# An attention kernel on one core: the small steps of gate and scales, and the masking of x, put into other batches

## The reference

```python
B, C, H, W = x.shape                       # 8, 512, 32, 32
pooled = jnp.mean(x, axis=(2, 3))
g = jax.nn.relu(pooled @ w1 + b1) @ w2 + b2
p = jax.nn.sigmoid(g)
mask = (p > 0.5).astype(x.dtype)
m = mask[:, :, None, None]
hyp_feat = x * m
euc_feat = x * (1.0 - m)
hyp_out = _logmap0(_mhsa(_expmap0(hyp_feat), hdn_w_qkv, hdn_b_qkv, hdn_w_o, hdn_b_o))
euc_out = _mhsa(euc_feat, eu_w_qkv, eu_b_qkv, eu_w_o, eu_b_o)
return hyp_out + euc_out
...
x = x + _L0_conv_ref(_gn(x), 1000, ...)    # _gn: group norm, 32 groups
```

## Time and profile before

| | us |
|---|---|
| median of 3 runs | 4210.61 (4202.07 to 4213.55) |
| the profiled execution: its time | 4202.53 |
| its span, first to last instruction | 4200.8 |
| PE busy in the span | 4004.4 (95%) |
| DVE busy | 2661.3 (63%) |
| POOL busy | 2693.4 (64%) |
| ACT busy | 1951.2 (46%) |

### The profile page before, as it was taken

The page is one execution under the profiler, slowest core; times in us unless marked ns, Lnnn a source line. Parts: engine busy times, 40 slices in busy tenths (PEclk is TensorE's granted clock), DMA queues, the critical chain, the costliest instruction groups (busy, mean ns, idle before and its releaser), DMA issues.

```text
span 4200.8 us, 68956 instructions
## 1 busy us (share of the span) xinstructions
PE 4004.4 (95%) x21822; PEld 2409.9 (57%) x21822; DVE 2661.3 (63%) x2643; ACT 1951.2 (46%) x3529; POOL 2693.4 (64%) x1311
## 2 busy tenths in 40 slices
PE   4899999999999999999999999999999999999999
PEld 3556565565655656556565555656556565555655
DVE  5565855658566684666746577465774657656585
ACT  4354534545345453454535445254553545435453
POOL 4474775747667486665857558574685746857477
PEclk9999999999999999999999999999999999999999
DMA  7212131121311213112141111311113111131212
...
DMA packets 143726, 306.49 MB, mean 73 GB/s; under 512 B 17248, under 2 KB 30048, under 8 KB 133088
## 3 DMA queue, kind: packets, MB, share of 16 engines
...
## 4 chain that ended last, share of the span: by engine, by line
PE 84%; DVE 9%; issue 4%; DMA 1%; ACT 1%; POOL 1%; SPq 0%; DVEq 0%; ACTq 0%; POOLq 0%
PE aux_ps L1220 30%; PE acc_ps L1331 20%; PE score_ps L1317 19%; PE aux_ps L1269 8%; PE score_ps L1220 4%; DVE mxp L1093 3%; PE aux_ps L1341 3%; DVE den L1154 1%; PE aux_ps L1278 1%; DVE o_t L1159 1%; DMA xin<-in_x_dram 1%; DVE sc L1000 0%; DVE keep L970 0%; DVE small L947 0%; DVE sc L907 0%
## 5 line engine op out<-in xcount | busy, mean ns | idle before, releaser
L628 POOL TENSOR_TENSOR sums<-sums,probs 128x1024 f32<-128x1024 f32 x768 | 1865.9, 2430 | 811.4 <-ACT probs L800 771.1
L1093 DVE TENSOR_REDUCE mxp<-aux_ps 128x2 f32<-128x1024 f32 x1031 | 1262.7, 1225 | 1094.6 <-PE aux_ps L1269 1068.7
L800 ACT ACTIVATE probs<-score_ps 128x512 f32<-128x512 f32 x2048 | 1056.5, 602 | 723.3 <-PE score_ps L1317 713.6
L1331 PE MATMUL acc_ps<-probs,v_y 128*64 128x512 f32 x4096 | 997.0, 608 | 0.0
L1220 PE MATMUL aux_ps<-xs,w_qk 128*128 128x512 f32 x3072 | 830.9, 408 | 0.0
L1220 PEld LDWEIGHTS aux_ps<-xs,w_qk 128*128 128x128 f32 x3072 | 542.3, 188 | 384.3 <-issue 267.9
L628 POOL TENSOR_TENSOR sums<-probs 128x1024 f32<-128x1024 f32 x128 | 305.0, 2383 | 501.3 <-ACT probs L800 501.3
L1269 PE MATMUL aux_ps<-k_hi,q_hi 64*128 64x512 f32 x2062 | 473.9, 453 | 102.5 <-DVE mxp L1093 100.7
L1331 PEld LDWEIGHTS acc_ps<-probs,v_y 128*64 128x64 f32 x4096 | 249.4, 136 | 468.4 <-issue 418.3
L1154 DVE RECIPROCAL den<-den 128x256 f32<-128x256 f32 (+1 forms) x240 | 443.9, 1850 | 7.7 <-ACT den L811 7.7
L1317 PE MATMUL score_ps<-q_hi,k_hi 64*128 64x512 f32 x2048 | 407.8, 394 | 17.9 <-issue 17.9
...
## 6 DMA issues: line engine op xcount, KB each, us to landing
...
xin<-in_x_dram SPq DMA_DIRECT2D x256, 256.0 KB, 2.9
...
```

The costliest lines, as they stand in the source:

```text
L628: pool.tensor_tensor(sums[h][:, :], a, probs[:, g % SLOTS_P, :], ALU.add).then_inc(c_sum[h].sem, 1)
L800: act.activation(probs[:, n % SLOTS_P, token_half(u % 2)], score_ps[:, u % SCORE_BANKS, :], ACT.Exp, scale=SCALE).then_inc(c_exp.sem, 1)
L1093: dve.tensor_reduce(mxp[:, :, n, h], ps, AX.X, ALU.max).then_inc(c_free["D"].sem, 1)
L1331: last = nc.tensor.matmul(acc_ps[head(j), :], v_y[:, m, head(2 * p + j)], probs[:, n % SLOTS_P, token_half(j)], start=(m == 0), stop=(m == ...
```

## The change

Four things are changed.

- The small steps of half 0 stand in other batches: statistics in 1 to 3 and none in 0, the group variance's product in 6 (was 5), the steps of the reciprocal deviation in 9, 10 and 11 (two of its parts now both in 9), the hidden layer in 12, the gate in 14, `ABOVE` in 17 (was 14), the masks (`KEEP`) in 25 (was 23) and `SHIFT` in 29.
- In half 1 the series is cut into five parts in batches 8, 9, 12, 13 and 14, and `BLEND` stands in 15 (was 14).
- The eight chunks of x go through by `MASK_AT`, in batches 15 (one), 16 (two), 17 (one), 19 (one), 20 (two) and 21 (one). ACT masks at the end of that batch, DVE scales a batch later, ACT makes the high part two batches later and POOL the low part at the start of the third.
- The ring has four buffers; the room comes from `squares`, whose work now alternates between two slots of `probs`, and from a narrower `mxw`.

```diff
-XIN = 3
+XIN = 4
-GATE_BATCH = {4: "mean", 5: "var", 11: "hidden", 13: "gate"}
-STATS_AT = {0: (0, 1), 1: (2, 3), 2: (4, 5), 3: (6, 7)}
-AGGREGATE, DEVIATIONS, RSTD_IN, RSTD, RELU, ABOVE, KEEP, SHIFT = 3, 5, 7, (8, 9, 10), 12, 14, 23, 24
+GATE_BATCH = {4: "mean", 6: "var", 12: "hidden", 14: "gate"}
+STATS_AT = {1: (0, 1, 2), 2: (3, 4, 5), 3: (6, 7)}
+AGGREGATE, DEVIATIONS, RSTD_IN, RSTD, RELU, ABOVE, KEEP, SHIFT = 3, 5, 7, (9, 10, 11), 13, 17, 25, 29
-CLAMP, POWER, SERIES, ROOT, NORM, EXP, SCALES, BLEND = 7, 8, (8, 11, 12), (9, 10), 11, 12, 13, 14
-OPERAND = [15, 16, 17, 18, 19, 20, 21, 22]
+CLAMP, POWER, ROOT, NORM, SERIES, EXP, SCALES, BLEND = 7, 8, (9, 10), 11, (8, 9, 12, 13, 14), 12, 13, 15
+MASK_AT = {15: (0,), 16: (1, 2), 17: (3,), 19: (4,), 20: (5, 6), 21: (7,)}
...
-        squares = sb("squares", [P, HALF])
-        mxw = sb("mxw", [P, NT, 66], F32R)
+        mxw = sb("mxw", [P, HD + NT], F32R)
...
             def x_lo(i, t, b):
-                if b - 1 in OPERAND:
-                    j = OPERAND.index(b - 1)
+                for j in MASK_AT.get(b - 3, ()):
...
                     for b in range(BATCHES):
+                        x_lo(i, t, b)
                         for g in (2 * b, 2 * b + 1):
...
                         if phase_at(b, MULT) is not None:
                             mult(phase_at(b, MULT))
-                        x_lo(i, t, b)
...
-                if b in OPERAND:
-                    operand_hi(i, t, OPERAND.index(b))
+                for j in MASK_AT.get(b, ()):
+                    mask(i, t, j)
...
                             exps(g)
-                        mask(i, t, b)
...
+                        for j in MASK_AT.get(b - 2, ()):
+                            operand_hi(i, t, j)
                         project(b)
...
-                if part < 2:
-                    root(i, part, small[:, 3, :], small[:, 2, :], small[:, 6, :])
+                    for n in range(2):
+                        root(i, n, small[:, 3, :], small[:, 2, :], small[:, 6, :])
...
-                if b in OPERAND:
-                    scale_x(i, t, OPERAND.index(b))
+                for j in MASK_AT.get(b - 1, ()):
+                    scale_x(i, t, j)
```

More of the change, by code:

```diff
@@ L75 @@
 RECIP, RECIP_PARTS = [6, 8], 4
+XIN_FIRST = ({"stats": 0, "w": 8, "operand": 12}, {"norm": 20, "operand": 28, "y": 36})
+NUMBERS = [first + j for kinds in XIN_FIRST for kind, first in kinds.items() for j in range(2 if kind == "w" else 8)]
 def max_slot_at(b, j):
@@ L394, in chunk_in, with y_square @@
             q = n % XIN
-            loads = (n - q) // XIN + 1
+            loads = 1 if t < 0 else len([c for c in NUMBERS if c <= n and c % XIN == q])
             eng.wait_ge(c_xin[q].sem, c_xin[q].at(i, 16 * loads))
             return xin_slot(t, kind, j)
+        def y_square(k):
+            return probs[:, SLOTS_P - 2 + k % 2, 0:HALF]
         def x_chunk(j):
@@ L413, in chunk_at @@
                 return 1 + j
-            first = ({"stats": 0, "w": 8, "operand": 10}, {"norm": 18, "operand": 26, "y": 34})[t]
-            return first[kind] + j
+            return XIN_FIRST[t][kind] + j
         def chunk_read(eng, i, t, kind, j):
@@ L539, in _ @@
                     if t:
-                        load_chunks(i, 1, "norm", range(5, 8), next_image)
-                        load_chunks(i, 1, "operand", range(3), next_image)
+                        load_chunks(i, 1, "norm", range(6, 8), next_image)
+                        load_chunks(i, 1, "operand", range(4), next_image)
                     load_qk(t, 3, 0)
@@ L675, in power, with mask @@
                 act.activation(dst, dst, ACT.Exp, scale=e).then_inc(made.sem, 1)
-            def mask(i, t, b):
-                if b in OPERAND:
-                    j = OPERAND.index(b)
-                    k, a = x_chunk(j)[0], 0 if new_image(t) else 1
-                    chunk = chunk_in(act, i, t, "operand", j)
-                    act.activation(chunk, chunk, ACT.Identity, bias=shift[:, a, k:k + 1],
-                                   scale=keep[:, a, k:k + 1]).then_inc(c_xm.sem, 1)
+            def mask(i, t, j):
+                k, a = x_chunk(j)[0], 0 if new_image(t) else 1
+                chunk = chunk_in(act, i, t, "operand", j)
+                act.activation(chunk, chunk, ACT.Identity, bias=shift[:, a, k:k + 1],
+                               scale=keep[:, a, k:k + 1]).then_inc(c_xm.sem, 1)
             def rstd_in(i):
@@ L899, in series @@
                 terms = [c / coefs[-1] for c in coefs[-2:0:-1]]
-                for n in ((0, 1), (2,), (3,))[part]:
-                    step(i, dve.scalar_tensor_tensor(dst, dst if n else s, terms[n], s, ALU.add, ALU.mult))
-                if part == 2:
+                if part < len(terms):
+                    step(i, dve.scalar_tensor_tensor(dst, dst if part else s, terms[part], s, ALU.add, ALU.mult))
+                else:
                     step(i, dve.tensor_scalar(dst, dst, coefs[-1], coefs[0], ALU.mult, ALU.add))
@@ L1069, in y_scale_step @@
                     step(i, dve.tensor_scalar(ss[:, :], ss[:, :], 1.0, None, ALU.min))
-                    for part in range(3):
+                    for part in range(5):
                         series(i, part, sc[:, 1, :], ss[:, :], ATANH_SERIES)
```

42 lines of the change are left out of this document (23 added, 19 removed).

## The result

The changed kernel takes **4165.7 us** (median of 4 runs, 4162.8 to 4168.1), the kernel before, run between them on the same chip, 4209.1 (4202.1 to 4213.6). The ratio is 0.990, with a 95% interval of 0.988 to 0.992. The forecast was 4192, with 4166 to 4214 as its range: the sign is right, the time lies 0.3 us under the range, and the gain is more than twice what was forecast. The two profiled executions say the same: spans of 4200.8 and 4161.1 us, 39.7 less, where the sum had 18. By the ratio's interval the gain is 36 to 50 us.

A forecast was written before the change was run, and what follows sets the result against it. PE, busy 95% at full clock, bounds the kernel with its work plus waits. Half 0 gains 4.2 us an image, half 1 loses 1.9: 18 for eight, 4202.5 to 4184; the runs' median lies 8 higher, 4192, range 4166 to 4214.

The forecast's parts named there:

- The rule of a wait: PE makes a batch's second pair of maxima only after DVE read the first; a read late by L costs L less 0.35.
- half 0's leaving costs: Half 0, per image: batch 5's wait of 2.3 to 2.5 us, batch 15's 1.0 and batch 24's 2.7 go.
- L955 in batch 10 and the multiplication in 11: Half 0: L955 behind batch 10's reciprocal keeps batch 11's 0.8 us; the last multiplication, behind batch 11's low part, costs 0.4.
- POOL's chain: POOL's low parts end 1.9 us later; in half 0 PE waits 1.3 in batch 20 and 1.0 in 24.
- Two scalings in a batch: Half 1, batches 17 and 21: two scalings delay the next read, costing 1.4 us in 18 and again in 22.
- Statistics leave batch 0, worth under 0.3 an image.: Half 0: moving the statistics out of batch 0 gains under 0.3 us an image.
- the change doesn't touch those: Waits of 0.7 and 1.2 us in the two batches 0, from the loop's turn and the last y tile's squares, stay.
- the ring's fourth buffer: Buffers for x: the fourth one, with the alternating squares, costs nothing, as no DMA held PE in the image shown.
- the series' parts in batches 9 to 14: Half 1: one more series step in batch 9 costs 0.3 to 0.5 us; one fewer in 11 wins 0.3.
- rival 1: The change does what it says and POOL's chain holds nobody: 5.8 us an image gained, 4164 us; chance 0.15.
- Rival 2: Slower: half 1's scalings in 18 and 22 miss a POOL sum, net loss 1.7 us an image, 4224 us; chance 0.14.
- rival 3: Nothing moves: half 1's new waits reach their upper bounds against the gate's savings, 4206 to 4210 us; chance 0.21.

The follow-up runs named there:

- e4: The kernel before with only half 0's statistics and the gate's steps moved, masks and half 1 as before: 4141.6 us, ratio 0.984.
- e8: The changed kernel with each ACT mask right behind the batch's exponentials, as in the kernel before, instead of at the batch's end: ratio 0.986.
- e7: The changed kernel with half 0's eight chunks of x back to one a batch, from batch 14 on: ratio 0.987.
- e9: The changed kernel with half 1's chunks one a batch, masks from batch 14 on and scalings from 15: ratio 0.988.
- e1: The kernel before with half 0's statistics alone moved to batches 1, 2 and 3: ratio 0.996.
- e2: The changed kernel with the statistics alone back in batches 0 to 3: ratio 0.994 to the kernel before.
- e3: The kernel before with the ring's fourth buffer, loads regrouped for it, squares in `probs` and the narrow `mxw`: ratio 0.998.
- e5: e4 with the ring's fourth buffer, the squares in `probs` and the narrow `mxw`: 4124.0 us, ratio 0.981 to the kernel before.
- e11: The kernel before with the squares in `probs` and the narrow `mxw`, but three buffers as before: ratio 1.000.
- e10: The changed kernel with half 1's small steps (series, `BLEND`) back where they stood before: ratio 0.989.
- e12: e5 with half 0's first five chunks one batch earlier and none worked on in batch 19: 4122.0 us, ratio 0.980 to the kernel before.

## Why the prediction was right or wrong

**Held.** *The rule of a wait and half 0's leaving costs*: batches 5, 15 and 24 lost 2.5, 1.0 and 2.7 us (e4), forecast 2.3 to 2.5, 1.0 and 2.7. `KEEP` in 25 and `ABOVE` in 17 hold nobody. *L955 in batch 10 and the multiplication in 11*: batches 10 to 14 together cost 0.5 an image more, forecast 0.4, and the wait in 11 stayed; but the 0.4 was to be a wait of PE in 12, and PE is idle there for 0.03 only, so the sum came right without its reason.

*POOL's chain*: PE waited 1.34 in image 3's batch 20, forecast 1.3, and 1.0 in 24, forecast 1.0. Counted from the start of batch 17 the chain to chunk 3 ended 2.0 later than before, forecast 1.9. The chain of the kernel after, POOL from batch 19 on:

```profile
1758.83 2.41 POOL L637 TENSOR_TENSOR sums<-sums,probs 128x1024 f32<-128x1024 f32 x1
1761.20 2.97 POOL L611 TENSOR_TENSOR xs<-xin,xs 128x512 fp32r<-128x512 f32 x2
1764.13 4.87 POOL L637 TENSOR_TENSOR sums<-sums,probs 128x1024 f32<-128x1024 f32 x2
1768.94 1.27 POOL L611 TENSOR_TENSOR xs<-xin,xs 128x512 fp32r<-128x512 f32 x1
```

and the q tile that starts when it ends:

```profile
1770.27 1.67 PE L1235 MATMUL aux_ps<-xs,w_qk 128*128 128x512 f32 x6 [1.34 <-POOL xs L611]
```

Of the 1.9 by which the chain was to end later, e8 showed the 0.7 of ACT's mask (0.65 came back), and with the chunks one a batch (e7) PE's wait for POOL in half 0 is gone.

*Two scalings in a batch*: forecast 1.4 in 18 and in 22, measured 1.43 and 1.34, and e9 took both away. DVE in batch 17 of half 1 (the two scalings, 2.49 and 2.89 by their single rows, and the read they delay):

```profile
2001.88 5.30 DVE L1029 TENSOR_TENSOR xin<-xin,sc 128x512 f32<-128x512 f32 x2
2007.10 1.21 DVE L1108 TENSOR_REDUCE mxp<-aux_ps 128x2 f32<-128x1024 f32 x1
```

POOL beside them:

```profile
2001.46 5.17 POOL L637 TENSOR_TENSOR sums<-sums,probs 128x1024 f32<-128x1024 f32 x2 [3.98 <-ACT probs L810]
```

Two sums fill 2001.46 to 2006.63, and each scaling ends a little behind one of them. The Trainium skill ("SBUF — State Buffer", section "Who interferes with whom") has a DVE instruction with two SBUF inputs and a GpSimd instruction that reads SBUF contend for a shared port pair that only one holds at a time; these rows agree.

**Wrong, the step that failed: "Statistics leave batch 0, worth under 0.3 an image."** With "the change doesn't touch those" of the waits at the loop's turn, and "the ring's fourth buffer ... I cost at nothing", it left 28 us out. The waits that the sum was made from were those of image 3, times eight. The longest wait of PE in the whole trace, 9.2 us, is in image 0, and the view of the whole span shows it in its first line ("longest 9.2"). The prediction went by that view for one image alone. What the runs showed in place of "under 0.3 an image": the statistics in batch 0 held DVE for the first load of x, 14 us at the turn (e1), 21 on top of the buffer (e2), and the fourth buffer, priced at nothing, was worth 8 to 18 (e3, e5, e11). Why the buffer is worth that is open.

**Wrong, the same habit: the clock.** Image 3 ran at full clock throughout, images 4 to 6 and 0 did not. Another 9.3 us of the kernel before, gone with the waits that they followed, and some 6.5 of the turn's 28 us are the clock too (batches 0, and image 0's batch 1). The prediction's "PE is busy 95% of the span at full clock", and the line ahead of it that the clock was granted in full throughout, are wrong: the mean was 0.993, and 0.998 in the kernel after.

**Mis-sized: half 1.** Forecast +15 us, measured +29 without the clock. Batches 18, 22 (22.2 us), 15 and 16 (-1.7) came as booked. Too small were: the series' parts in batches 9 to 14, +8.2 instead of +0.4 to 1.6 (the sum's remainder, or its 0.5 less 0.3 an image); batch 24's chain, +5.0 instead of +0.8; and batch 20, which won 3.9 and was to win 6.8. The first is a term that I priced by its own length: "one more series step in batch 9, 0.3 behind two that wait". DVE, half 1, batch 9:

```profile
1947.35 1.47 DVE L907 TENSOR_TENSOR sc<-sc 128x128 f32<-128x128 f32 x1
1948.85 2.44 DVE L908 TENSOR_TENSOR sc<-sc,ss 128x128 f32<-128x128 f32 x1
1951.33 1.26 DVE L916 SCALAR_TENSOR_TENSOR sc<-sc,ss 128x128 f32<-128x128 f32 x1
1952.71 1.23 DVE L1108 TENSOR_REDUCE mxp<-aux_ps 128x2 f32<-128x1024 f32 x1
```

The third step, L916, took 1.26, for POOL had begun another operation between it and L908:

```profile
1951.10 1.35 POOL L644 TENSOR_TENSOR o_raw<-o_raw,den 128x512 f32<-128x512 f32 x1
```

The rows were there to be read: L970 and L971 "both waited, one behind the other" is the prediction's own rule, and it was not applied to this term. e10 gave 8.1 of these us back, of which batches 15 and 16 took 1.6.

**The rivals.** The time is that of rival 1 (4164), but not its reason: PE waits for POOL 32 times. Rival 2 didn't come: there are no waits in 19 and 23. Nor did rival 3, by its time (4206 to 4210), though it was right that half 1's new waits eat up much of the gate's savings. That the time lies only 0.3 us under the range owes more to luck than the two halves deserve: they lost 16 us against the forecast, and the turn and the clock, which were not in the sum, won 37. The measured time is a sum of what the forecast said, 14 us more loss in half 1, 2 more in half 0, 28 won at the turn and 9 by the clock in batches 3 to 30: -18 + 14 + 2 - 28 - 9 = -39. The working was sound where it looked, and looked at one image of eight.

**A better kernel.** e5, the moves of statistics and gate with the ring, and without the rest, takes 4124.0 us (4119.0 to 4124.9), ratio 0.981 (0.979 to 0.983), 42 under the changed kernel's median (37 by the ratios, each to the kernel before run beside it); e12 the same within what can be told. Between e5 and the kernel after, batches 20 and 24 of half 0 lose 13.2 us, 18 and 22 of half 1 22.2, batches 9 to 16 6.5 and 24 5.0; batch 20 wins 3.7.
